# Seven chained attentions on one core: a score slot or a maxima item becomes four heads over both row halves of the array, written to a pair of PSUM banks and drained by one instruction

## The chip, the cores and the metric

One NeuronCore of a Trainium2 chip. The time is device microseconds (us) of one execution, the median of the runs taken; lower is better. TensorE (PE) multiplies, VectorE (DVE) and ScalarE (ACT) read its results out of PSUM, GpSimd (POOL) does small side work, SyncE (SP) issues the DMAs.

## The reference, cut to what matters

Four batches of 256 rows with 160 columns pass through seven attentions and two gated feed-forward blocks. Attentions 0, 2 and 6 read 512 context rows with 20 heads of 8 columns, attentions 1 and 5 are self-attentions over 256 rows with 20 heads of 8, attention 3 reads 508 context rows with 8 heads of 20, and attention 4 has 96 query rows over 256 keys with 8 heads of 20. Each is

```
q = (x @ wq).reshape(b, n, heads, dh).transpose(0, 2, 1, 3)
sim = jnp.einsum('bhid,bhjd->bhij', q, k) * scale
a = jax.nn.softmax(sim, axis=-1)
out = jnp.einsum('bhij,bhjd->bhid', a, v)
x = out @ wo + bo + residual
```

The softmax needs the largest score of each query row and head.

## The kernel before

All work is cut into steps, and `plan()` writes one order of 3015 steps for all engines before the program is built. Each engine walks that order and takes its own part of each step, with semaphores between the engines. `simulate()` makes the order greedily: it keeps a model clock for each engine (`cost()`), due times that are counted in score slots (`PV_LAG`, `K_LEAD`, `M_LEAD`, `FIRST_W`, `BG_LEAD`, `TAIL`), and looks ahead 12 us before it lets TensorE change its shape.

Heads are handled in quads of four. For a quad there are:

- `max` steps (L1024 on PE, L1504 on DVE): scores with the queries as rows of the result, into one bank of 512 fp32 columns; DVE reduces the bank to the row maxima `mx`. With 512 or 508 keys one head fills a bank, with 256 keys two heads do. There are 720 such steps.
- `negm` and `mtr` (L1518, L1519, L1038, L1528): the negated maxima are transposed and added to the query rows, so that the scores of the next step come out already lowered.
- `st` steps, the score slots (L1004 on PE, L1326 on ACT): transposed scores of two heads, 128 keys by 256 queries each, into one bank; ACT writes their exp to one of `N_P = 8` slots of `probs`. There are 736.
- `pv` steps (L1064): four heads' probabilities of a 128-key chunk times the values, into the eighth bank `pv_ps`; `oev` (L1335) reads that out. There are 368 `pv` steps of eight matmul records each.

Heads of a quad lie two on partitions 0 to 63 and two on 64 to 127 (`half`, `same_half`). Score and maxima matmuls contract over 64 rows only, so each uses one half of the array's rows, and matmuls on the two halves can run at once. All heads of one `st` or one `max` step are of the same half, and successive steps alternate halves.

TensorE thus works in three shapes: "rows" (`st` and `max`, 64-row halves), "columns" (`pv`, four 32-column groups) and "full" (all else: projections, transposes, feed-forward, `mtr`). Seven banks `bank_ps` are shared by all steps but `pv`: the planner gives each step any of the seven (`banks_of`), the drain of the step frees it (`bank_taken`), and PE waits for that before it writes the bank again (`take`).

Before the first matmul of an `st` or `max` step, and thus behind a mode change or not, PE waits for its bank:

```python
                def take(step):

                    b, k = turn[step]
                    if k:
                        pe.wait_ge(bank_taken[b], k)
                    return bank_ps[b], bank_full[b]
```

Of the kernel before, what the change touches and what calls it, by code (L numbers as in the profile page):

```python
# [38 lines left out]
P = 128  # L39
# [26 lines left out]
N_P = 8  # L66
RING = 4
RUN = 1
PV_LAG = 2
FIRST_W = 3  # L70
K_LEAD = 4
TAIL = 40
BG_LEAD = 11
M_LEAD = 8
# [128 lines left out]
def plan():  # L203

    quads, slots, span = [], [], []
    for ph, us in enumerate(PHASES):
        for b in range(B):
            first = len(slots)
            for u in us:
                a = ATT[u]  # L210
                n_c = -(-a["nk"] // P)
                for qd in range(a["H"] // 4):
                    n, start = len(quads), len(slots)
                    for c in range(n_c):
                        for k, heads in enumerate(same_half(u, qd)):
                            slots.append(dict(n=n, u=u, b=b, c=c, heads=heads, last=c == n_c - 1 and k == 1))
# [34 lines left out]
    for k in range(len(PHASES) * B):  # L251
        ph, b = divmod(k, B)
        lists = before(ph, b)
        spread(span[k - 1][0] - lead if k else -80, span[k][0] - lead, spread_lists(lists))
# [49 lines left out]
def cost(step, quads):  # L304
# [17 lines left out]
    if kind == "max":  # L322
        rows = a["hpm"] * nk
        return 0.455 * rows, [("dve", 60 + 1.05 * rows)]
# [4 lines left out]
    if kind == "st":  # L329
        return 0.458 * a["hps"] * a["nq"], act(a["hps"] * a["nq"])  # L330
# [38 lines left out]
PATIENCE = 800  # L369
OTHERS = 0.1  # L370
# [13 lines left out]
def simulate(quads, slots, due, stages):  # L384
# [38 lines left out]
    def data_needs(step):  # L423
# [13 lines left out]
        if kind == "st":  # L437
            s = step[1]
            return [("mtr", slots[s]["n"])] + ([pv_of[s - N_P]] if s >= N_P else [])
# [52 lines left out]
    def facts(step):  # L492

        if step not in info:
            pe, after = cost(step, quads)
            side = None
            if step[0] == "st":
                side = half(slots[step[1]]["u"], slots[step[1]]["heads"][0])
            if step[0] == "max":
                side = half(quads[step[1]]["u"], quads[step[1]]["items"][step[2]][2][0])  # L500
            shape = "rows" if step[0] in ("st", "max") else "columns" if step[0] == "pv" else "full"
            info[step] = (needs(step), pe, after, shape, side, takes_buffer(step), due.get(step, (-10**6, 0, 0)), banks_of(step))
        return info[step]

    class State:
# [34 lines left out]
        def choices(self):  # L540

            out = []
            for step, home in list(self.firsts()):
                need, pe, _, shape, side, lock, rank, banks = facts(step)
# [6 lines left out]
                else:  # L551
                    free = seen = max(self.clock["pe"], self.lanes[side] if shape == "rows" else max(self.lanes))
                bank = None
                if banks:
                    open_at = [(0 if self.banks[i] is None else self.at(self.banks[i]), i) for i in banks]
                    open_at = [x for x in open_at if x[0] is not None]
# [3 lines left out]
                    t, bank = max(ready) if ready else min(open_at)  # L560
# [4 lines left out]

        def take(self, choice):

            _, start, free, home, step, bank = choice
            _, pe, after, shape, side, lock, _, _ = facts(step)
# [23 lines left out]
            if bank is not None:  # L593
                self.banks[bank] = ("low", step) if step[0] in LOW else step
# [39 lines left out]
BANKED = SPARE | {"st", "max"}  # L634


def banks_of(step):

    return range(N_BANK) if step[0] in BANKED else ()

# [25 lines left out]
def build(nc, io):  # L666
    order, place, quads, slots = plan()

    value, seen, turn, uses = {}, {}, {}, N_BANK * [0]
    for step in order:  # L670
# [7 lines left out]
        if step[0] in BANKED:  # L678
            turn[step] = (place[step], uses[place[step]])
            uses[place[step]] += 1  # L680

    with ExitStack() as ctx:
# [8 lines left out]
        bank_ps = [ctx.enter_context(nc.psum_tensor(f"bank_ps{i}", [P, 512], F32)) for i in range(N_BANK)]  # L691
# [58 lines left out]
        probs = sb("probs", [P, N_P, 512])  # L750
        gate = sb("gate", [P, FC, SQ])
# [1000 lines left out]
```

## Time and profile before

| | |
|---|---|
| median of 3 runs | 930.72 us (930.34 to 931.19) |
| the profiled execution: its own time | 930.49 us |
| its span, first to last instruction | 928.7 us |
| around the span | 1.8 us |
| PE / DVE / ACT busy | 874.5 / 690.4 / 655.9 us |
| mean granted TensorE clock | 0.98 |

A busy share is a union of overlapping records: matmul records overlap each other, so a PE that is busy for 94% can still be held up between two matmuls. How far it is held up is read from the starts of successive matmuls in the timeline.

### The profile page before, as it was taken

Reading aid. Unit: us, or ns where it says so; the run is one execution under the profiler, and the core shown is the slowest. Engines: PE = TensorE matmul, PEld = TensorE weight load, DVE = VectorE, ACT = ScalarE, POOL = GpSimd, SP = SyncE. Lnnn points to the kernel's source line nnn. Section 1 sums busy time; section 2 is a strip of 40 time slices with the busy share of each in tenths; the row PEclk is TensorE's granted clock in tenths of the full one; section 3 lists DMA queues with packets and bytes.
Section 4 is the critical chain, followed back from the end, with each engine's and each line's share of the span. In section 5 each row is a group of like instructions: output and inputs, shape, how many; then the busy total and the mean of one; then the engine's idle time right before and its main releaser. Section 6 shows DMA issues by size and latency. Waiting matters only on the chain.

```text
span 928.7 us, 21290 instructions
## 1 busy us (share of the span) xinstructions
PE 874.5 (94%) x7810; PEld 592.9 (64%) x7810; DVE 690.4 (74%) x1653; ACT 655.9 (71%) x1419; POOL 56.3 (6%) x98
## 2 busy tenths in 40 slices
PE   8999999999999998989999899999899999898986
PEld 6656655666666666666667666666666656556664
DVE  4978888878888875866867676867788978586813
ACT  8777786877777866776768586677777767667551
POOL 2000000000001000000000000000000000000100
PEclk9999999999999999999999999999999999989989
DMA  8111221111111110111000200101112111111000
GB/s 244 38 38 36 66 58 35 25 29 25 27 38 35 35 28 20 24 35 24 12 2 2 75 2 1 24 18 47 53 28 53 25 36 35 31 23 40 15 8 8
DMA packets 26829, 32.55 MB, mean 35 GB/s; under 512 B 9316, under 2 KB 17768, under 8 KB 26728
## 3 DMA queue, kind: packets, MB, share of 16 engines
q1 hardware_dynamic: 26728, 31.19, 13.3%
q8 instruction: 65, 1.06, 0.5%
q14 instruction: 36, 0.29, 0.1%
HBM read 9.54 MB, written 0.66 MB: 11 GB/s over the span
## 4 chain that ended last, share of the span: by engine, by line
PE 72%; ACT 11%; DVE 10%; issue 5%; SPq 1%; DMA 0%; ACTq 0%; POOL 0%; POOLq 0%; DVEq 0%
PE pv_ps L1064 16%; PE bank_ps L1024 12%; PE bank_ps L1004 10%; ACT probs L1326 5%; DVE mx L1504 5%; PE bank_ps L1111 5%; PE bank_ps L980 4%; PE bank_ps L981 4%; PE bank_ps L1193 3%; PE bank_ps L1091 3%; PE bank_ps L1038 3%; PE bank_ps L1241 3%; PE bank_ps L1181 2%; PE bank_ps L1230 2%; ACT L1439 1%
## 5 line engine op out<-in xcount | busy, mean ns | idle before, releaser
L1504 DVE TENSOR_REDUCE mx<-bank_ps 128x1 f32<-128x512 f32 (+3 forms) x720 | 452.8, 682 | 80.3 <-PE bank_ps L1024 78.7
L1326 ACT ACTIVATE probs<-bank_ps 128x512 f32<-128x512 f32 x736 | 381.1, 605 | 108.8 <-PE bank_ps L1004 107.0
L1064 PE MATMUL pv_ps<-probs,v_all 128*9 128x256 f32 (+2 forms) x2944 | 202.0, 378 | 4.1 <-ACT probs L1326 2.5
L1024 PE MATMUL bank_ps<-ring,qT 64*128 64x512 f32 (+1 forms) x800 | 170.2, 402 | 7.9 <-issue 3.3
L1004 PE MATMUL bank_ps<-qT,ring 64*128 64x256 f32 x1280 | 170.9, 305 | 2.3 <-DVE qT L1528 0.7
L1004 PEld LDWEIGHTS bank_ps<-qT,ring 64*128 64x128 f32 x1280 | 129.8, 186 | 51.3 <-issue 18.8
L1024 PEld LDWEIGHTS bank_ps<-ring,qT 64*128 64x128 f32 x800 | 88.2, 186 | 59.2 <-issue 29.9
L1064 PEld LDWEIGHTS pv_ps<-probs,v_all 128*9 128x9 f32 (+2 forms) x2944 | 57.6, 91 | 75.8 <-issue 21.4
L1377 ACT ACTIVATE kdense<-bank_ps 128x512 fp32r<-128x512 f32 (+2 forms) x116 | 58.7, 560 | 22.6 <-PE bank_ps L1111 22.5
L1111 PE MATMUL bank_ps<-identr,ks 128*128 128x128 f32 (+1 forms) x416 | 61.0, 281 | 8.1 <-DVE gate L1617 4.6
L1301 ACT ACTIVATE ks<-bank_ps 128x320 fp32r<-128x320 f32 x80 | 35.7, 446 | 46.4 <-PE bank_ps L1091 25.3
L1528 DVE TENSOR_TENSOR qT<-bank_ps,qT 128x256 fp32r<-128x256 f32 (+1 forms) x108 | 47.2, 437 | 23.9 <-PE bank_ps L1038 23.3
L1111 PEld LDWEIGHTS bank_ps<-identr,ks 128*128 128x128 f32 (+1 forms) x416 | 52.2, 191 | 17.5 <-DVE gate L1617 4.9
L1335 ACT ACTIVATE oT<-pv_ps 128x256 f32<-128x256 f32 x108 | 43.4, 402 | 22.4 <-PE pv_ps L1064 22.1
L1038 PE MATMUL bank_ps<-identr,mn 128*128 128x128 f32 (+1 forms) x248 | 53.3, 302 | 1.9 <-DVE mn L1519 1.0
L1038 PEld LDWEIGHTS bank_ps<-identr,mn 128*128 128x128 f32 (+1 forms) x248 | 37.9, 192 | 26.8 <-issue 9.5
L1230 PE MATMUL bank_ps<-hx,up 128*128 128x256 f32 x320 | 44.1, 290 | 4.8 <-DVE qT L1528 2.8
L1230 PEld LDWEIGHTS bank_ps<-hx,up 128*128 128x128 f32 x320 | 40.0, 190 | 8.9 <-DVE qT L1528 3.0
L1193 PE MATMUL bank_ps<-ident,oT 128*128 128x128 f32 x216 | 35.6, 300 | 10.2 <-ACT oT L1335 10.1
L1682 POOL TENSOR_SCALAR rstd<-mv 128x2 f32<-128x2 f32 x24 | 5.2, 217 | 657.8 <-DVE mv L1550 657.8
L1605 DVE TENSOR_TENSOR x<-bank_ps,xb 128x320 f32<-128x320 f32 x30 | 14.7, 490 | 33.1 <-PE bank_ps L1241 20.2
L1426 ACT ACTIVATE qT<-bank_ps 128x512 fp32r<-128x512 f32 (+1 forms) x68 | 34.0, 552 | 6.6 <-PE bank_ps L1181 6.1
(188 smaller groups left out, 1032.5 us busy)
## 6 DMA issues: line engine op xcount, KB each, us to landing
ring<-kdense SPq DMA_DIRECT2D x240, 64.0 KB, 2.0
ring<-kdense SPq DMA_DIRECT2D x160, 32.0 KB, 1.9
gate<-in_w_up SPq DMA_DIRECT2D x4, 640.0 KB, 4.4
wb<-in_w_blk SPq DMA_DIRECT2D x2, 960.0 KB, 5.3
wd<-in_w_down SPq DMA_DIRECT2D x2, 400.0 KB, 5.5
x<-in_x SPq DMA_DIRECT2D x4, 160.0 KB, 4.2
bias<-in_bias SPq DMA_DIRECT2D x1, 640.0 KB
out_rows<-x SPq DMA_DIRECT2D x4, 160.0 KB, 1.9
```

Of the source, the lines that this page charges most:

```text
L1004: mm = pe.matmul(bank[0:kr, i * a["nq"]:(i + 1) * a["nq"]], key_op(n, h)[:, c * P:c * P + kr], query_rows(u, b, h), start=True, stop=True)
L1024: mm = pe.matmul(bank[0:rows, j * a["nk"]:(j + 1) * a["nk"]], query_rows(u, b, h)[:, tt * P:tt * P + rows], key_op(n, h)[:, 0:a["nk"]], st ...
L1038: mm = pe.matmul(bank[:, k * a["nq"] + i * P:k * a["nq"] + i * P + rows], m, identr[0:rows, 0:rows], start=True, stop=True)
L1064: mm = pe.matmul(pv_ps[32 * j:32 * j + a["dh"] + 1, 0:a["nq"]], v, probs[0:kr, s % N_P, i * a["nq"]:(i + 1) * a["nq"]], start=(c == 0), st ...
L1111: mm = pe.matmul(bank[:, k * SQ + t * P:k * SQ + t * P + kr], ks[0:kr, t, g * of(u):(g + 1) * of(u), :].rearrange("p h s -> p (h s)"), ide ...
L1193: mm = pe.transpose(bank[0:rows, k * P:(k + 1) * P], src, ident[:, :])
L1230: mm = pe.matmul(bank[:, k * SQ:(k + 1) * SQ], up[:, w, lo:lo + P], hx[:, h, :], start=(j == 0), stop=(j == len(terms) - 1))
L1326: nc.scalar.activation(probs[0:kr, s % N_P, 0:w], bank[0:kr, 0:w], ACT.Exp, scale=float(a["dh"]) ** -0.5).then_inc(free, 1)
L1335: nc.scalar.activation(dst, pv_ps[:, 0:ATT[u]["nq"]], ACT.Copy).then_inc(S["out_taken"], 1)
L1377: nc.scalar.activation(dst, bank[:, 0:n * SQ].rearrange("p (g k) -> p g k", g=n)[:, :, 0:w], ACT.Copy).then_inc(free, 1)
L1504: nc.vector.tensor_reduce(mx[b][0:rows, t, heads[0]:heads[-1] + 1:heads[-1] - heads[0] or 1], bank[0:rows, 0:a["hpm"] * a["nk"]].rearrange ...
L1528: nc.vector.tensor_tensor(q, bank[:, 0:(g1 - g0) * nq], q.bitcast(F32), ALU.add).then_inc(done, 1)
```

## The change

A score slot and a maxima item now hold both halves: `slots` get `heads=same_half(u, qd)`, two lists of two heads, and `items_of` gives for each row tile one item with heads of both halves. So there are 368 `st` and 360 `max` steps in place of 736 and 720, each with twice the matmuls. The matmuls are issued alternately to half 0 and half 1, half 0 into the first bank of a pair and half 1 into the second. The seven banks are three pairs and a lone one; `st` and `max` may only go to a pair, and need both of its banks free, while every other step takes any single bank, by preference the lone one or one whose partner is in use (`alone`). One exp of two times 512 columns and one maximum over two banks drain a pair. `probs` holds the same bytes, as four double slots. On PE, `take` waits for the last user of each of the two banks; each bank's last matmul raises the same semaphore, which is waited for at two more. The due-time constants are halved, since they count slots. The number and the form of the matmuls stay, `pv` too.

```diff
-PV_LAG = 2
-FIRST_W = 3
-K_LEAD = 4
-TAIL = 40
-BG_LEAD = 11
-M_LEAD = 8
+N_D = 4
+N_PAIR = 3
+PV_LAG = 1
+FIRST_W = 2
+K_LEAD = 2
+TAIL = 20
+BG_LEAD = 6
+M_LEAD = 4
...
-    per = [[(t, rows, hs[i:i + a["hpm"]]) for i in range(0, 2, a["hpm"]) for t, rows in tiles] for hs in same_half(u, qd)]
-    return [item for both in zip(per[1], per[0]) for item in both]
+    return [(t, rows, i, [hs[i:i + a["hpm"]] for hs in same_half(u, qd)]) for i in range(0, 2, a["hpm"]) for t, rows in tiles]
...
-                        for k, heads in enumerate(same_half(u, qd)):
-                            slots.append(dict(n=n, u=u, b=b, c=c, heads=heads, last=c == n_c - 1 and k == 1))
+                        slots.append(dict(n=n, u=u, b=b, c=c, heads=same_half(u, qd), last=c == n_c - 1))
...
-        return 0.455 * rows, [("dve", 60 + 1.05 * rows)]
+        return 0.455 * rows, dve(2 * rows)
...
-        return 0.458 * a["hps"] * a["nq"], act(a["hps"] * a["nq"])
+        return 0.458 * a["hps"] * a["nq"], act(2 * a["hps"] * a["nq"])
...
-                if shape == "rows":
-                    self.lanes[side], self.clock["pe"] = t, begin + (pe / 2 if step[0] == "st" else 0)
-                else:
-                    self.lanes, self.clock["pe"] = [t, t], t
-                self.work += pe / 2 if shape == "rows" else pe
+                self.lanes, self.clock["pe"] = [t, t], t
+                self.work += pe
...
+        def alone(self, i, t):
+
+            if i >= 2 * N_PAIR:
+                return True
+            other = self.banks[i ^ 1]
+            return other is not None and (self.at(other) or LATE) > t
...
-    return range(N_BANK) if step[0] in BANKED else ()
+    return range(0, 2 * N_PAIR, 2) if step[0] in DOUBLE else range(N_BANK) if step[0] in BANKED else ()
+
+
+def banks_used(step, i):
+
+    return (i, i + 1) if step[0] in DOUBLE else (i,)
...
-                    b, k = turn[step]
-                    if k:
-                        pe.wait_ge(bank_taken[b], k)
-                    return bank_ps[b], bank_full[b]
+                    for owner in owners[step]:
+                        taken(pe, owner)
+                    return bank_of(step), bank_full[place[step]]
...
-                        for i, h in enumerate(sl["heads"]):
-                            mm = pe.matmul(bank[0:kr, i * a["nq"]:(i + 1) * a["nq"]],
-                                           key_op(n, h)[:, c * P:c * P + kr], query_rows(u, b, h),
-                                           start=True, stop=True)
-                        mm.then_inc(full, 1)
+                        for i in range(2):
+                            for k in range(2):
+                                h = sl["heads"][k][i]
+                                mm = pe.matmul(bank[0:kr, k, i * a["nq"]:(i + 1) * a["nq"]],
+                                               key_op(n, h)[:, c * P:c * P + kr], query_rows(u, b, h),
+                                               start=True, stop=True)
+                                if i == 1:
+                                    mm.then_inc(full, 1)
...
-                        nc.scalar.activation(probs[0:kr, s % N_P, 0:w], bank[0:kr, 0:w], ACT.Exp,
+                        nc.scalar.activation(pair_probs[0:kr, s % N_D, :, 0:w], bank[0:kr, :, 0:w], ACT.Exp,
                                              scale=float(a["dh"]) ** -0.5).then_inc(free, 1)
...
-                        nc.vector.tensor_reduce(mx[b][0:rows, t, heads[0]:heads[-1] + 1:heads[-1] - heads[0] or 1],
-                                                bank[0:rows, 0:a["hpm"] * a["nk"]].rearrange("p (h k) -> p h k", k=a["nk"]),
+                        qd, hpm = quads[n]["qd"], a["hpm"]
+                        m = mx[b][0:rows, t, 4 * qd:4 * qd + 4].rearrange("p (s j) -> p s j" if a["sr"] == 32 else "p (j s) -> p s j", s=2)
+                        nc.vector.tensor_reduce(m[:, :, i:i + hpm], bank[0:rows, :, 0:hpm * a["nk"]].rearrange("p s (h k) -> p s h k", k=a["nk"]),
                                                 AX.X, ALU.max).then_inc(free, 1)
```

## Rows read from the trace of the kernel before

**Rows 1.** The page, busy time of each engine: us, share of span, instructions.

```profile
PE 874.5 (94%) x7810; PEld 592.9 (64%) x7810; DVE 690.4 (74%) x1653; ACT 655.9 (71%) x1419; POOL 56.3 (6%) x98
```

**Rows 2.** The page, chain that ended last, shares of the span.

```profile
PE 72%; ACT 11%; DVE 10%; issue 5%; SPq 1%; DMA 0%; ACTq 0%; POOL 0%; POOLq 0%; DVEq 0%
PE pv_ps L1064 16%; PE bank_ps L1024 12%; PE bank_ps L1004 10%; ACT probs L1326 5%; DVE mx L1504 5%; PE bank_ps L1111 5%; PE bank_ps L980 4%; PE bank_ps L981 4%; PE bank_ps L1193 3%; PE bank_ps L1091 3%; PE bank_ps L1038 3%; PE bank_ps L1241 3%; PE bank_ps L1181 2%; PE bank_ps L1230 2%; ACT L1439 1%
```

**Rows 3.** PE timeline, whole span, first and last score or maxima run: start us, us.

```profile
23.08 1.75 PE L1024 MATMUL bank_ps<-ring,qT 64*128 64x512 f32 x8 [0.57 <-issue]
...
900.30 0.95 PE L1004 MATMUL bank_ps<-qT,ring 64*128 64x256 f32 x4
```

**Rows 4.** PE timeline, undisturbed score or maxima runs and the row behind each.

```profile
252.21 0.50 PE L1004 MATMUL bank_ps<-qT,ring 64*128 64x256 f32 x2
252.64 0.40 PE L1064 MATMUL pv_ps<-probs,v_all 128*9 128x256 f32 x4
...
506.96 0.50 PE L1004 MATMUL bank_ps<-qT,kdense 64*128 64x256 f32 x4
507.39 0.41 PE L1064 MATMUL pv_ps<-probs,v_all 124*21 124x256 f32 x4
...
680.09 0.74 PE L1004 MATMUL bank_ps<-qT,ring 64*128 64x256 f32 x8
680.76 0.40 PE L980 MATMUL bank_ps<-wb,hT_in 128*128 128x160 f32 x1
```

**Rows 5.** PE timeline, a run of seven slots and items, and the row behind.

```profile
836.27 0.74 PE L1004 MATMUL bank_ps<-qT,ring 64*128 64x256 f32 x8
836.85 0.84 PE L1024 MATMUL bank_ps<-ring,qT 64*128 64x512 f32 x3
837.96 0.40 PE L1064 MATMUL pv_ps<-probs,v_all 128*9 128x256 f32 x4 [0.27 <-ACT oT L1335]
```

**Rows 6.** PE timeline, two visits to `pv` (one and three steps), each with the row behind.

```profile
146.58 0.62 PE L1064 MATMUL pv_ps<-probs,v_all 128*9 128x256 f32 x8
147.13 0.39 PE L1004 MATMUL bank_ps<-qT,ring 64*128 64x256 f32 x2
...
99.06 1.48 PE L1064 MATMUL pv_ps<-probs,v_all 128*9 128x256 f32 x24
100.47 0.39 PE L1004 MATMUL bank_ps<-qT,ring 64*128 64x256 f32 x2
```

**Rows 7.** Lines by form, drains: busy us, mean ns | idle before, releaser.

```profile
L1326 ACT ACTIVATE probs<-bank_ps 128x512 f32<-128x512 f32 x688 | 364.1, 617 | 102.7 <-PE bank_ps L1004 101.1
L1326 ACT ACTIVATE probs<-bank_ps 128x192 f32<-128x192 f32 x32 | 9.3, 339 | 5.6 <-PE bank_ps L1004 5.6
L1504 DVE TENSOR_REDUCE mx<-bank_ps 128x1 f32<-128x512 f32 x480 | 301.2, 683 | 48.2 <-PE bank_ps L1024 47.0
L1528 DVE TENSOR_TENSOR qT<-bank_ps,qT 128x256 fp32r<-128x256 f32 x100 | 41.7, 417 | 22.6 <-PE bank_ps L1038 22.1
L1528 DVE TENSOR_TENSOR qT<-bank_ps,qT 128x512 fp32r<-128x512 f32 x8 | 5.5, 687 | 1.3 <-PE bank_ps L1038 1.2
```

**Rows 8.** Timelines of DVE and ACT, drains one behind another.

```profile
49.70 3.67 DVE L1504 TENSOR_REDUCE mx<-bank_ps 128x1 f32<-128x512 f32 x6
...
377.60 3.06 ACT L1326 ACTIVATE probs<-bank_ps 128x512 f32<-128x512 f32 x6
```

**Rows 9.** Views of L1326 and L1504, who waited for it: us, times (largest).

```profile
  PEld bank_ps L1024: 12.7, 24
  PEld bank_ps L1004: 11.0, 31
  PEld pv_ps L1064: 9.1, 27
...
  PEld bank_ps L1004: 9.8, 26
  PEld bank_ps L1024: 9.1, 22
```

**Rows 10.** View of L975, PE's waits that stand as instructions of their own: ns min/median/max.

```profile
L975 PEldq EVENT_SEMAPHORE  x232: 51/51/3063, 21.7 to 894.7; - x116
```

More of the change, by code:

```diff
@@ L369 @@
 PATIENCE = 800
+LATE = 10**9
 OTHERS = 0.1
@@ L495, in facts @@
             pe, after = cost(step, quads)
[L496 to L500, printed above, removed]
             shape = "rows" if step[0] in ("st", "max") else "columns" if step[0] == "pv" else "full"
-            info[step] = (needs(step), pe, after, shape, side, takes_buffer(step), due.get(step, (-10**6, 0, 0)), banks_of(step))
+            info[step] = (needs(step), pe, after, shape, takes_buffer(step), due.get(step, (-10**6, 0, 0)), banks_of(step))
         return info[step]
@@ L543, in choices @@
             for step, home in list(self.firsts()):
-                need, pe, _, shape, side, lock, rank, banks = facts(step)
+                need, pe, _, shape, lock, rank, banks = facts(step)
                 times = [self.at(x) for x in need]
@@ L551, in choices @@
                 else:
-                    free = seen = max(self.clock["pe"], self.lanes[side] if shape == "rows" else max(self.lanes))
+                    free = seen = max(self.lanes)
                 bank = None
                 if banks:
-                    open_at = [(0 if self.banks[i] is None else self.at(self.banks[i]), i) for i in banks]
-                    open_at = [x for x in open_at if x[0] is not None]
+                    open_at = [(max(0 if self.banks[j] is None else self.at(self.banks[j]) or LATE for j in banks_used(step, i)), i) for i in banks]
+                    open_at = [x for x in open_at if x[0] < LATE]
                     if not open_at:
@@ L559, in choices @@
                     ready = [x for x in open_at if x[0] <= max(start, seen)]
-                    t, bank = max(ready) if ready else min(open_at)
+                    t, bank = max(ready, key=lambda x: (self.alone(x[1], max(start, seen)), x)) if ready else min(open_at)
                     start = max(start, t)
@@ L564, in choices @@
             return out
+        def alone(self, i, t):
[3 more added lines that the diff above has]
+            return other is not None and (self.at(other) or LATE) > t
         def take(self, choice):
             _, start, free, home, step, bank = choice
-            _, pe, after, shape, side, lock, _, _ = facts(step)
+            _, pe, after, shape, lock, _, _ = facts(step)
             if home[0] == "stream":
@@ L593, in take @@
             if bank is not None:
-                self.banks[bank] = ("low", step) if step[0] in LOW else step
+                for j in banks_used(step, bank):
+                    self.banks[j] = ("low", step) if step[0] in LOW else step
         def worth(self, choice):
@@ L678, in build @@
         if step[0] in BANKED:
-            turn[step] = (place[step], uses[place[step]])
-            uses[place[step]] += 1
+            b = place[step]
+            turn[step] = (b, uses[b])
+            uses[b] += 1
+            fills[b] += 2 if step[0] in DOUBLE else 1
+            full_at[step] = fills[b]
+            owners[step] = [user[j] for j in banks_used(step, b) if j in user]
+            for j in banks_used(step, b):
+                user[j] = step
     with ExitStack() as ctx:
@@ L690, in build, with bank_of @@
         pv_ps = ctx.enter_context(nc.psum_tensor("pv_ps", [P, 512], F32))
-        bank_ps = [ctx.enter_context(nc.psum_tensor(f"bank_ps{i}", [P, 512], F32)) for i in range(N_BANK)]
+        pair_ps = [ctx.enter_context(nc.psum_tensor(f"pair_ps{i}", [P, 2, 512], F32)) for i in range(N_PAIR)]
+        lone_ps = [ctx.enter_context(nc.psum_tensor(f"lone_ps{i}", [P, 512], F32)) for i in range(N_BANK - 2 * N_PAIR)]
+        bank_ps = [pair[:, i, :] for pair in pair_ps for i in range(2)] + [lone[:, :] for lone in lone_ps]
+        def bank_of(step):
+            return pair_ps[place[step] // 2] if step[0] in DOUBLE else bank_ps[place[step]]
         wm = sb("wm", [P, 2, 640])
@@ L936, in _ @@
                         if before is not None:
[L938 to L939 removed]
+                            scored = ("st", quads[before]["slots"][-1])
+                            sp.wait_ge(bank_full[place[scored]], full_at[scored])
                         for j in range(4):
@@ L1011, in _ @@
                         a = ATT[u]
-                        t, rows, heads = quads[n]["items"][i]
+                        t, rows, _, heads = quads[n]["items"][i]
                         if i == 0:
@@ L1283, in filled @@
             def filled(eng, step):
-                b, k = turn[step]
-                eng.wait_ge(bank_full[b], k + 1)
-                return bank_ps[b], bank_taken[b]
+                b = place[step]
+                eng.wait_ge(bank_full[b], full_at[step])
+                return bank_of(step), bank_taken[b]
             def high_slots(stack, t0, t1, rows, dh, which):
```

38 lines of the change are left out of this document (21 added, 17 removed).

## The prediction

> **What bounds the kernel now.** I read the engines' busy time first, then the chain of work that ended last, then TensorE's timeline. No engine is full: PE has 94%, DVE 74%, ACT 71% [rows 1]. The chain spends 72% of the span on PE, 11% on ACT and 10% on DVE, and the two drains that the change touches, exp (L1326) and maximum (L1504), have 5% each of it [rows 2]. So the order in which PE is fed decides, and most of a gain must come from PE's own time or from its waits for banks.
>
> PE's time in the "rows" shape is in its timeline. I split the timeline wherever PE leaves `st` and `max` for another shape. That gives 310 runs (the first and the last are shown [rows 3]), with 235 visits to `pv` and 219 stretches of full shape between them. From the first matmul of each run to the first matmul behind it the 310 runs take 314 us together. What an undisturbed run costs is seen in three of them: one slot alone takes 0.43 us (252.21 to 252.64), two slots on different halves also 0.43 (506.96 to 507.39), four slots 0.67 (680.09 to 680.76) [rows 4]. So a run costs 0.195 us once, and 0.235 us for each two slots that lie on different halves; **an odd slot costs as much as a pair**, since the other half of the array stands idle. Of the 310 runs 154 have an odd number of slots and items (26 have one, 29 three, 37 five, 55 seven, 6 nine, 1 thirteen). Taking for each run the fuller half, in units of 512 columns, gives 806 units; both halves always full would be 718.
>
> The 314 us are then 310 x 0.195 = 60 us of entering, 718 x 0.235 = 169 us of work with both halves, 88 x 0.235 = 21 us for the idle halves, and 64 us left, which are waits for banks. A run of seven shows them: by these numbers it should take 0.195 + 4 x 0.235 = 1.14 us and takes 1.69 (836.27 to 837.96) [rows 5].
>
> **The change part by part, against the profiled execution** (930.5 us with the 1.8 around its 928.7 us span; the median is 0.2 above it, so the same sum holds for the median).
>
> *Both halves in every step.* The 88 units of idle half go: -20.7 us. This is PE's own time, not hidden by anything: PE's order is one stream. Where a run ended in a wait for a bank the gain is swallowed; where not, it counts in full. I take it in full here and put the waits below.
>
> *One drain for two banks.* In a row of six, a maximum follows the last at (3.67 - 0.68) / 5 = 0.598 us and an exp at (3.06 - 0.61) / 5 = 0.491 us [rows 8]. No row shows a drain of 1024 columns. The nearest rows give the cost of further columns: exp (617 - 339) / 320 = 0.87 ns each, DVE (687 - 417) / 256 = 1.05 ns each [rows 7]. A double exp in a row is then at most 491 + 512 x 0.87 = 936 ns in place of 982, a double maximum 598 + 540 = 1138 in place of 1196. Alone, without a drain ahead of it, the double exp is 617 + 445 = 1062 against 617 + 491 = 1108. So each engine gains some 50 ns a pair: 368 x 0.05 = 18 us of ACT and 360 x 0.058 = 21 us of DVE. Only what is on the chain counts: 5% and 5% of 928.7 are 46 us each, and 5% of these is -4.6 us together. The bounds are 0 (the second bank's columns cost a restart) and -9 (all waits of PE for these drains shrink as well [rows 9]). A double drain begins no later than now: the two matmuls of a slot on one half take 0.235 us in series, and the four of a double, two on each half, take the same.
>
> The Trainium skill (ScalarE: Activation LUTs, the passage on the length of an ACTIVATE) gives 186 ns + 0.833 ns a column and an overlap of 93 ns back to back. That is 613 ns for 512 columns, and the trace has 617. By it a pair of exps in a row would save 93 ns rather than 46, and the sum would be about 2 us lower; the sum keeps the rows.
>
> *Banks in pairs.* This is the debit side. A double holds both banks until the whole drain ends, where now the first bank is free one drain earlier (0.49 or 0.60 us). A full-shape step that sits in one bank of a pair makes the partner useless to `st` and `max`. With three pairs no run can hold more than three doubles without waiting, against seven slots now; 78 of the 310 runs have seven or more. The due planner reacts by leaving the shape earlier, which means more runs. One more run costs 0.195 us to enter, and the visit it splits costs another entry: `pv` takes 0.55 us for one step (146.58 to 147.13) and 1.41 for three (99.06 to 100.47), so 0.43 a step and 0.12 an entry [rows 6]. One more run is therefore about 0.32 us. Now there are 1456 / 2 / 310 = 2.35 pairs a run. The lower bound for the price is no more runs (a mean of 2.35 doubles fits under three). The upper one is a mean of 1.75, 416 runs, +106 x 0.32 = +34 us. I take 25 more runs, a mean of 2.17, +8 us: nearer to the lower end because the runs of one odd slot go and because the halves' waste was in the long runs too. The 64 us of waits I leave as they are, since faster drains and scarcer banks pull opposite ways; one fifth either way, 13 us, is for the range.
>
> The Trainium skill (TensorEngine Tiling (Array Packing), PSUM Bottleneck and Gotcha 1) speaks against the change: tiling speeds up the array, not the emptying of PSUM, and row tiling raises the pressure on banks since the halves must write different ones. The 64 us of waits agree. By that rule alone the 21 us would turn into waits; what this does here is the third rival.
>
> *Waits on PE.* Each `st` and `max` now waits for two banks, so one wait more of the kind that stands as an instruction of its own. 232 such exist at the first step of a quad, 51 ns at the median [rows 10]; about 500 more come. At a median of 51 ns the wait itself is already over when it is reached, and it can be passed while earlier matmuls still run. Cost between 0 and 500 x 0.051 = +25 us; I take +2.
>
> *Hidden.* ACT and DVE get fewer instructions and waits, `pv`, `mtr`, projections and feed-forward keep their matmuls. The ring's DMAs on SP wait for the last score slot of the quad four earlier as now. The constants are halves of the old ones in slots that are twice as large, so the leads stay; I cost them at nothing, and if a lead came out short the chain would show `mx` or `ring` waits at quad starts. `probs` keeps its bytes.
>
> **Sum**: 930.5 - 20.7 - 4.6 + 8 + 2 = 915.2; I say 915.
>
> **The rivals.**
> 1. *Waits shrink as well* (12%). PE records waits for exp and maxima in front of L1024, L1004 and L1064 of 9 to 13 us each [rows 9]. If fewer, larger drains and an exact lane model cut them, and no runs are added: 930.5 - 20.7 - 9 - 13 = 888 at the far end, 895 typically. For it: the old order was partly made of slots that used one half. Against it: pairs are scarcer than banks.
> 2. *The idle halves were free* (16%). Where a run ends because the next bank is taken, a half slot less only lengthens the wait. With the shorter time eaten up by 60 more runs, or by waits, the result is 926 to 934. For it: the 64 us of waits lie mostly in the long runs, 40 us in those of six and more. Against it: the 55 runs of one or three slots show almost no wait, 4 us.
> 3. *Bank pairs run out* (17%). Full-shape steps leave only two usable pairs, runs shrink under 1.9 doubles, and PE switches shape more often. It decides from 25.3 / 0.32 = 79 more runs, 389 in all, 1.87 doubles a run; at 1.75 and with the waits up by a fifth it is 930.5 - 25.3 + 34 + 2 + 13 = 954, typically 942. This is the one that ends slower.
> 4. *The second wait is exposed* (5%). 500 x 0.051 us where PE has eight instructions to issue in the 0.235 us of a double: 915 + 23 = 938.
>
> **How the numbers follow.** The forecast has 50%, with its own range of 903 to 926 (the bounds of the drains, 0 to 50 more runs, half of the waits' fifth). The rivals have 12, 16, 17 and 5%. A range of 893 to 943 leaves out a little of rivals 1 and 3, some 15%. Faster by over 0.2% (below 928.9) takes the forecast, rival 1 and a part of rival 2: 0.63. Within 0.2%, about what a measurement of this kernel can tell from no change: 0.08. Slower: the rest of rival 2, with rivals 3 and 4: 0.29.
>
> **What the profile after would show.** Right: the undisturbed run with one double at 0.43 us and with two at 0.67; no run with L1004 x2 or a lone L1024 of 512 columns; 310 to 360 runs, together under 300 us; exp near 1.05 us and maximum near 1.22 us each, ACT and DVE busy time 15 to 25 us lower each; PE's span share up. Wrong: more than 389 runs, or the time of the runs at 314 us or more, with PE waiting for `probs` or `mx` (rival 2 or 3); gaps of 0.05 us and more behind the extra wait instructions inside a run (rival 4). The forecast falls if the planner cannot keep two doubles a run.

## The result, and the profile after

The changed kernel takes 951.31 us (948.42 to 955.60, four runs) against 930.96 us (930.34 to 932.01) before: a ratio of 1.0221, 95% interval 1.0181 to 1.0262. It is slower, where faster was forecast; whether by more than 2% the interval leaves open. 951 lies outside the range. The profiled execution took 951.76 us with a span of 950.0.

The page after, busy time and chain:

```profile
PE 869.3 (92%) x7810; PEld 566.9 (60%) x7810; DVE 669.8 (71%) x1293; ACT 638.4 (67%) x1051; POOL 56.4 (6%) x98
...
PE 72%; ACT 11%; DVE 10%; issue 6%; DMA 1%; SPq 0%; POOLq 0%; DVEq 0%; ACTq 0%; POOL 0%
```

Against [rows 1, 2] every engine has less to do (DVE -20.6 us, ACT -17.5) and the span is 21 us longer, so each waits more: PE's idle time, its span less its busy time, is 80.7 us against 54.2. The chain's shares have hardly moved, which already says that they were a poor guide to what an engine's time is worth.

PE's timeline, first the undisturbed runs that answer to [rows 4] with the row behind each (one double of maxima, two doubles of slots), then the first and last run:

```profile
563.84 0.49 PE L1048 MATMUL pair_ps<-kdense,qT 64*128 64x508 f32 x2
564.26 0.54 PE L1117 MATMUL pair_ps<-wc,ctxT 128*128 128x320 f32 x1
...
272.79 0.74 PE L1025 MATMUL pair_ps<-qT,ring 64*128 64x256 f32 x8
273.46 0.40 PE L1090 MATMUL pv_ps<-probs,v_all 128*9 128x256 f32 x4
...
22.90 0.50 PE L1048 MATMUL pair_ps<-ring,qT 64*128 64x512 f32 x2 [0.46 <-DMA ring<-kdense]
...
922.04 0.50 PE L1025 MATMUL pair_ps<-qT,ring 64*128 64x256 f32 x4
```

A double takes 0.42 us, two take 0.67, as predicted. There are 356 runs (112 of one double, 125 of two, 114 of three, 5 longer) with 257 visits to `pv` and 245 stretches of full shape from the first run on. The spans between first matmuls, by shape (before has 218 stretches of full shape by this count; the prediction had 219):

| | before | after | |
|---|---|---|---|
| 310 / 356 score and maxima runs | 314.2 us | 305.9 | -8.3 = -20.7 idle halves, +9.0 entries, +3.4 other (waits inside) |
| 235 / 257 visits to `pv` | 192.3 | 214.1 | +21.8, of which 22 x 0.12 = 2.6 are entries |
| 218 / 245 stretches of full shape | 396.1 | 404.1 | +8.0 |

The gain is where it was looked for. Of the signs named beforehand two did not come: the runs take 305.9 us and not under 300, and PE's share of the span fell from 94% to 92%. The loss is in the *other* shapes: by this count a visit to `pv` reaches to the first matmul behind it, and where that is a double that waits for its pair, the wait is counted there. The worst such place, in the timelines of PE, ACT and DVE:

```profile
858.36 0.64 PE L1256 MATMUL pair_ps<-hx,up 128*128 128x256 f32 x4
...
858.92 1.05 PE L1090 MATMUL pv_ps<-probs,v_all 128*9 128x256 f32 x16
859.42 1.27 ACT L1465 ACTIVATE gate<-gate 128x1280 f32<-128x1280 f32 x1
...
860.80 0.87 DVE L1644 SCALAR_TENSOR_TENSOR gate<-pair_ps,cols,gate 128x256 f32<-128x256 f32 x2 [4.88 <-ACT gate L1465]
...
861.92 0.86 DVE L1644 SCALAR_TENSOR_TENSOR gate<-lone_ps,cols,gate 128x256 f32<-128x256 f32 x2
862.71 0.47 DVE L1644 SCALAR_TENSOR_TENSOR gate<-pair_ps,cols,gate 128x256 f32<-128x256 f32 x1
...
863.33 0.79 PE L1025 MATMUL pair_ps<-qT,ring 64*128 64x256 f32 x4 [3.35 <-DVE gate L1644]
```

The feed-forward's `ff_a` results sit in single banks of pairs until the gelu is done; the next score double needs a whole pair, and PE stands idle for 3.35 us. Such long ones are few, and the feed-forward is not the main cause: PE's recorded idle time right in front of a score or maxima run adds up to 4.0 us before and 20.6 after, of which the trace puts 6.2 down to maxima, 6.1 to exps and 6.1 to the feed-forward's L1644. The Trainium skill (TensorEngine Tiling (Array Packing), PSUM Bottleneck and Gotcha 1) holds that tiling speeds up the array and not the emptying of PSUM, and that it raises the pressure on banks; this trace agrees, with the 12.3 us of waits for maxima and exps. Counted more widely, gaps of over 0.04 us beyond the undisturbed change of shape add up to 41 us before and 67 after; of these the ones in front of a score or maxima run go from 9.3 us (40 places) to 29.8 (92 places).

**The clock.** The granted clock is 0.971 in the profiled run after, 0.980 before. TensorE drops from 2.4 to 1.2 GHz in stretches of 3.4 to 6.8 us before and 3.4 to 10.2 after, 37.5 and 54.6 us in all. The windows of the last 130 to 150 us, after and before (PE, PEld, DVE, ACT, POOL busy us and instructions, then granted clock):

```profile
800.00:950.00 150.00, 123.84 (x1034) 81.40 (x1033) 83.28 (x158) 78.16 (x104) 7.83 (x12) 0.91 0.10 23
```

```profile
800.00:928.70 128.70, 109.55 (x910) 75.33 (x910) 73.19 (x173) 70.00 (x136) 7.84 (x12) 0.93 0.09 23
```

In both, PE is busy for only 83 to 85% there and the clock is lowest; elsewhere it is busy for 92 to 96% with a clock of 0.96 to 1.00. **Span times granted clock** turns out to be the steadier measure of a kernel here: 19 executions of before on one chip, with clocks from 0.970 to 0.989, lay between 920.7 and 938.8 us, and their product between 907.5 and 912.2. The two slowest of them, 934.9 and 938.8 us, count as slow and are left out from here on; the median product of the other 17 is 909.0. After has 922.9 (921.5 to 924.8). By this measure 13.9 us of the loss is work and waits, and the rest, some 7 us, goes with the lower clock. I call this product "at full clock" below and use it to tell parts apart, beside the times.

It is a yardstick and not a time that any run took, and it has a lean. Over the 19 executions the span falls by 8.5 us for each 0.01 of clock, where a constant product would want 9.5, so a kernel whose clock is 0.02 lower comes out some 2 us too good (an estimate). Nor does it say what lowers the clock: if a kernel's own waits do, the lost time is its cost all the same.

### The profile page after: what moved, and what is told of

Its sections match the earlier page's. It is cut to its first block, busy times and chain, and to the rows that moved or that the text cites. A ratio compares the mean times of both kernels' runs of the same rounds, so it can differ in the third digit from the quotient of the medians.

```text
span 950.0 us, 20809 instructions
## 1 busy us (share of the span) xinstructions
PE 869.3 (92%) x7810; PEld 566.9 (60%) x7810; DVE 669.8 (71%) x1293; ACT 638.4 (67%) x1051; POOL 56.4 (6%) x98
## 4 chain that ended last, share of the span: by engine, by line
PE 72%; ACT 11%; DVE 10%; issue 6%; DMA 1%; SPq 0%; POOLq 0%; DVEq 0%; ACTq 0%; POOL 0%
PE pv_ps L1090 15%; PE pair_ps L1048 11%; PE pair_ps L1025 11%; DVE mx L1532 6%; ACT probs L1352 5%; PE lone_ps L999 3%; PE pair_ps L1137 3%; PE lone_ps L1267 2%; PE lone_ps L1000 2%; PE pair_ps L1117 2%; PE lone_ps L1137 2%; PE pair_ps L1207 2%; PE pair_ps L1219 2%; PE lone_ps L1256 1%; PE pair_ps L1063 1%
## 5 line engine op out<-in xcount | busy, mean ns | idle before, releaser
L1532 DVE TENSOR_REDUCE mx<-pair_ps 128x2 f32<-128x1024 f32 (+3 forms) x360 | 430.0, 1218 | 110.0 <-PE pair_ps L1048 107.9
L1352 ACT ACTIVATE probs<-pair_ps 128x1024 f32<-128x1024 f32 x368 | 360.2, 1003 | 158.9 <-PE pair_ps L1025 157.8
L1048 PE MATMUL pair_ps<-ring,qT 64*128 64x512 f32 (+1 forms) x800 | 145.0, 405 | 20.1 <-DVE mx L1532 5.7
L1025 PE MATMUL pair_ps<-qT,ring 64*128 64x256 f32 x1280 | 143.2, 313 | 17.9 <-DVE gate L1644 7.8
L1025 PEld LDWEIGHTS pair_ps<-qT,ring 64*128 64x128 f32 x1280 | 102.2, 189 | 77.9 <-issue 36.4
L1048 PEld LDWEIGHTS pair_ps<-ring,qT 64*128 64x128 f32 x800 | 70.6, 187 | 76.7 <-issue 42.9
L1403 ACT ACTIVATE kdense<-pair_ps 128x512 fp32r<-128x512 f32 (+2 forms) x69 | 34.4, 538 | 13.9 <-PE pair_ps L1137 13.7
L1137 PE MATMUL pair_ps<-identr,ks 128*128 128x128 f32 x244 | 37.6, 284 | 1.1 <-DVE mx L1532 0.4
L1137 PEld LDWEIGHTS pair_ps<-identr,ks 128*128 128x128 f32 x244 | 32.3, 196 | 4.5 <-DVE mx L1532 2.3
L1137 PE MATMUL lone_ps<-identr,ks 128*128 128x128 f32 (+1 forms) x172 | 30.0, 293 | 0.7 <-DVE ks L1493 0.7
L1063 PEld LDWEIGHTS lone_ps<-identr,mn 128*128 128x128 f32 (+1 forms) x118 | 17.7, 190 | 19.8 <-issue 13.3
```

The source lines that it names most:

```text
L1025: mm = pe.matmul(bank[0:kr, k, i * a["nq"]:(i + 1) * a["nq"]], key_op(n, h)[:, c * P:c * P + kr], query_rows(u, b, h), start=True, stop=True)
L1048: mm = pe.matmul(bank[0:rows, k, j * a["nk"]:(j + 1) * a["nk"]], query_rows(u, b, h)[:, tt * P:tt * P + rows], key_op(n, h)[:, 0:a["nk"]], ...
L1063: mm = pe.matmul(bank[:, k * a["nq"] + i * P:k * a["nq"] + i * P + rows], m, identr[0:rows, 0:rows], start=True, stop=True)
L1137: mm = pe.matmul(bank[:, k * SQ + t * P:k * SQ + t * P + kr], ks[0:kr, t, g * of(u):(g + 1) * of(u), :].rearrange("p h s -> p (h s)"), ide ...
L1352: nc.scalar.activation(pair_probs[0:kr, s % N_D, :, 0:w], bank[0:kr, :, 0:w], ACT.Exp, scale=float(a["dh"]) ** -0.5).then_inc(free, 1)
L1403: nc.scalar.activation(dst, bank[:, 0:n * SQ].rearrange("p (g k) -> p g k", g=n)[:, :, 0:w], ACT.Copy).then_inc(free, 1)
```

## The experiments

Each is timed beside before on the same chip, in four groups: e1 to e4; e5, e6, b1 and a1; f0, f2, fa and e7; e8 to e10. The table's row of before is that of the second group; at full clock before had 911.0, 909.0, 909.5 and 908.9 in the four. Median time, ratio to before with its interval, and the median at full clock:

| | form | us | ratio | clock | full clock |
|---|---|---|---|---|---|
| before | | 930.1 | | 0.980 | 909.0 |
| after | pairs, held, one drain | 951.3 | 1.022 (1.018-1.026) | 0.971 | 922.9 |
| e1_adjacent | any neighbours, held, one drain | 952.7 | 1.025 (1.018-1.032) | 0.975 | 927.4 |
| e2_halves_only | any two, own release, two drains | 946.6 | 1.017 (1.011-1.023) | 0.959 | 906.1 |
| e3_two_drains | pairs, held, two drains | 972.3 | 1.046 (1.040-1.051) | 0.965 | 935.6 |
| e4_one_wait | after with one wait | 946.5 | 1.018 (1.014-1.022) | 0.973 | 918.3 |
| e5_any_two_held | any two, held, two drains | 939.7 | 1.012 (1.009-1.016) | 0.976 | 917.9 |
| e6_pairs_own | pairs, own release, two drains | 943.0 | 1.012 (1.003-1.020) | 0.982 | 923.6 |
| b1_patience | before, another order | 924.8 | 0.994 (0.991-0.997) | 0.982 | 905.1 |
| a1_patience | after, nearly the same order | 951.9 | 1.021 (1.015-1.027) | 0.971 | 922.9 |
| e7_halves_patience | e2, another order | 949.7 | 1.023 (1.019-1.027) | 0.959 | 908.5 |
| f0_before_short | before, short drains | 883.9 | 0.951 (0.947-0.956) | 0.987 | 870.0 |
| f2_halves_short | e2, short drains | 889.9 | 0.954 (0.946-0.961) | 0.971 | 862.8 |
| fa_after_short | after, short drains | 892.0 | 0.961 (0.958-0.963) | 0.981 | 874.0 |
| e8_ff_banks | after, `ff_a` in the last three banks | 955.8 | 1.025 (1.017-1.033) | 0.971 | 926.1 |
| e9_ff_banks_one_wait | e8 with one wait | 949.5 | 1.021 (1.015-1.027) | 0.970 | 918.5 |
| e10_any_two_one_wait | e5 with one wait | 935.7 | 1.006 (1.002-1.010) | 0.981 | 915.6 |

**Which part costs.** The first group.

e1: the double's banks are any two neighbours of the seven; the planner's rule for which free bank to prefer is fitted to that.

```diff
+                    if step[0] in DOUBLE:
+                        when = {i: x for x, i in open_at}
+                        open_at = [(max(when[i], when[i + 1]), (i, i + 1)) for i in range(N_BANK - 1) if i in when and i + 1 in when]
...
```

> The changed kernel with any two neighbouring banks of the seven for a double (six positions in place of three) and still one drain for both. If it is the fixed pairing of banks that costs the time (theory A), the waits in front of a score or maxima run fall and the time comes to 935 to 945 us. If it is that two banks are held together for the length of a double drain, wherever they lie (theory B), or the planner's order with steps twice as large (theory C), it stays at 945 to 955. Its planned order has 361 score and maxima runs against 356.

e2: any two banks, each with its own drain and semaphores.

```diff
-                        nc.scalar.activation(pair_probs[0:kr, s % N_D, :, 0:w], bank[0:kr, :, 0:w], ACT.Exp,
-                                             scale=float(a["dh"]) ** -0.5).then_inc(free, 1)
+                        for k, (at, count) in enumerate(turn[step]):
+                            act.wait_ge(bank_full[at], count + 1)
+                            nc.scalar.activation(pair_probs[0:kr, s % N_D, k, 0:w], bank_ps[at][0:kr, 0:w], ACT.Exp,
+                                                 scale=float(a["dh"]) ** -0.5).then_inc(bank_taken[at], 1)
...
```

> Only the first half of the change: a slot or item has four heads on both array halves, but in any two of the seven banks, each with its own drain of 512 columns and its own semaphores, so that a bank is free as soon as its own drain ends. Theories A and B (banks in pairs, held together) expect 912 to 930 us, the gain of the full halves without its price. Theory C (larger steps make a worse order) expects 945 or more. 329 runs are planned.

e3: the order and banks of after, two drains (the maximum likewise).

```diff
+                        for k in range(2):
+                            ins = nc.scalar.activation(pair_probs[0:kr, s % N_D, k, 0:w], bank[0:kr, k, 0:w], ACT.Exp,
+                                                       scale=float(a["dh"]) ** -0.5)
+                        ins.then_inc(free, 1)
...
```

> The changed kernel in the very same order and banks, but each double drained by two instructions of 512 columns, the pair freed behind the second. It measures what one drain for two banks gives: by the 46 to 58 ns a pair of the prediction and a chain share of 10 to 11% for the two drains the time should be 5 to 10 us above the changed kernel, 956 to 961 us. If the double instruction were slower than two (theory D), it would be below 951.

e4: the order and banks of after, no wait twice.

```diff
-            owners[step] = [user[j] for j in banks_used(step, b) if j in user]
+            owners[step] = list(dict.fromkeys(user[j] for j in banks_used(step, b) if j in user))
```

> The changed kernel in the same order and banks, but where both banks of a pair were last used by the same step, PE waits once and not twice. If the extra wait instructions hold PE up (rival 4 of the prediction), some us come off, up to 0.051 us for each wait left out; theories A to C expect no change, 948 to 954 us.

e1 brought nothing, so three fixed positions are no worse than six neighbouring ones, and theory A as it was worded for e1 (fixed positions) falls. e2 surprised: with free banks and own release it still takes 946.6 us. At full clock it is 2.9 under the table's before (4.9 under the 911.0 of its own group); its clock is the lowest of all, 0.959. Its stretch from 100 to 200 us shows it, and before's beside it:

```profile
100.00:200.00 100.00, 90.57 (x772) 51.70 (x768) 72.18 (x162) 65.98 (x138) 3.58 (x6) 0.85 0.13 32
```

```profile
100.00:200.00 100.00, 96.82 (x912) 59.45 (x904) 80.50 (x187) 74.58 (x157) 3.51 (x6) 1.00 0.18 45
```

e2's longest stretch at 1.2 GHz is 23.9 us, and in the 6.8 us ahead of it PE was busy for 4.23:

```profile
130.30:137.10 6.80, 4.23 (x46) 1.89 (x38) 6.70 (x13) 2.45 (x5) 0.00 (x0) 1.00 0.18 41
137.10:161.00 23.90, 22.30 (x132) 13.56 (x136) 14.02 (x27) 12.22 (x25) 0.00 (x0) 0.50 0.10 23
```

But the clock is not all that e2 loses. The busy times on its page:

```profile
PE 870.2 (92%) x7810; PEld 568.3 (60%) x7810; DVE 687.5 (73%) x1653; ACT 654.6 (69%) x1419; POOL 56.6 (6%) x98
```

In its span of 945.6 us PE is idle for 75.4 us, against 54.2 before. Two costs in this are not of the halves as such. First, e2 keeps the second wait of each double: PE's waits that stand as instructions of their own number 965 in before, 1576 in after and 1846 in e2. Second, its order holds one long stop, of which 5.46 us are recorded as idle before a matmul. PE, the view of L995, where PE waits in `take` (its longest wait, 5.96 us, is this one), and SP there:

```profile
358.01 0.62 PE L1092 MATMUL pv_ps<-probs,v_all 128*9 128x256 f32 x8
364.09 1.22 PE L1050 MATMUL all_ps<-ring,qT 64*128 64x512 f32 x4 [5.46 <-issue]
...
L995 PEldq EVENT_SEMAPHORE  x843: 51/51/5963, 22.0 to 906.3; - x169
...
359.75 0.28 SPq L926 DMA_DIRECT2D ca_n<-in_ctx  x1
360.13 4.94 SPq L962 DMA_DIRECT2D ring<-kdense  x8
```

PE needs keys from the ring, and SP issues their transfers only behind a small load of attention 4's context rows (L926), which by SP's program waits until a VectorE step (L1498, 359.41 us) has freed its bank. So a late transfer, and not a bank, stops the kernel there. Before has no idle place of PE over 2.8 us.

e3 showed the single drain to be worth 21 us of time and 12.7 at full clock in this order, several times the forecast. PE's idle time is 90.2 us in it, 80.7 in after. The order was planned with the cost of one drain, so a plan made for two might lose less; that was not tried with pairs held. The busy times on e3's page, then the top two groups by line and form of e3, then those of after (busy us, mean ns of one, idle time before them and its releasers):

```profile
PE 877.4 (91%) x7810; PEld 570.3 (59%) x7810; DVE 692.2 (72%) x1653; ACT 660.6 (68%) x1419; POOL 56.5 (6%) x98
```

```profile
L1353 ACT ACTIVATE probs<-pair_ps 128x512 f32<-128x512 f32 x688 | 366.2, 605 | 144.1 <-PE pair_ps L1025 142.3
L1535 DVE TENSOR_REDUCE mx<-pair_ps 128x1 f32<-128x512 f32 x480 | 301.5, 683 | 60.6 <-PE pair_ps L1048 59.3
```

```profile
L1352 ACT ACTIVATE probs<-pair_ps 128x1024 f32<-128x1024 f32 x344 | 344.4, 1026 | 145.9 <-PE pair_ps L1025 144.9
L1532 DVE TENSOR_REDUCE mx<-pair_ps 128x2 f32<-128x1024 f32 x240 | 286.4, 1218 | 66.9 <-PE pair_ps L1048 65.4
```

ACT's and DVE's busy time differ by 22 us each, as the 18 and 21 of the forecast said; a double exp takes 1.026 us, a double maximum 1.218. The Trainium skill (ScalarE: Activation LUTs, the passage on the length of an ACTIVATE) gives 186 ns + 0.833 ns a column, 1039 ns for 1024 columns; the trace has 1026.

e4 is 4.8 us of time and 4.6 at full clock under after. PE's separate waits of the `taken` helper, after and in e4:

```profile
L896 PEldq EVENT_SEMAPHORE  x1230: 51/51/2952, 10.9 to 943.1; - x176
```

```profile
L896 PEldq EVENT_SEMAPHORE  x737: 51/51/3180, 11.8 to 937.8; - x185
```

493 waits of 51 ns less gave 4.6 us, 9 ns each: most are covered, but not all. After was timed in another group than e4, and before moved by 2 us between groups, so the size is rough; e9 against e8, in one group, gives 7.6 us for 492 waits, 15 ns each. At 9 ns the 881 waits that e2 has more than before would cost some 8 us, an estimate.

**Position or holding, and how much is the order.** The second group. e5 is e2 with both banks given back behind the second drain, e6 is e3 with each bank given back behind its own; the planner reckons with it in both. b1 and a1 change one number of the planner, `PATIENCE = 700`, in before and in after.

> As e2_halves_only (any two of the seven banks, two drains of 512 columns), but both banks are given back together, behind the second drain. If what costs is that the first bank is held through the drain of the second (theory B), the time is near that of e3_two_drains, 962 to 975 us. If it is the fixed pairs (theory A), it is near e2_halves_only, 942 to 952 us. 361 score and maxima runs are planned, against 329 of e2_halves_only.

> As e3_two_drains (fixed pairs of banks, two drains of 512 columns), but each bank is given back behind its own drain, and the planner reckons with that. Theory B expects about what e2_halves_only has, 942 to 952 us; theory A stays near e3_two_drains, 962 to 975 us. 335 runs are planned.

> The kernel before, with the planner's PATIENCE at 700 in place of 800 and nothing else: another order of the same steps (296 score and maxima runs in place of 310). It shows how far two orders of the same kernel lie apart. If the difference between before and after is a lucky order of before (theory C in its strong form), this is some 940 us or more; if the orders are alike, 925 to 937 us.

> The changed kernel with PATIENCE at 700 in place of 800: another order of the same steps (356 runs, as many as after has). If the order of the changed kernel is an unlucky one, this comes to 935 to 943 us; if the loss is in the change itself, 945 to 957 us.

By the times alone e5 and e6 fit neither theory, because e2 and e3, between which they stand, have the lowest clocks. At full clock the four forms with two drains make a square:

| at full clock | own release | held together |
|---|---|---|
| any two banks | 906.1 (e2) | 917.9 (e5) |
| pairs | 923.6 (e6) | 935.6 (e3) |

Holding costs 11.8 and 12.0, pairs 17.5 and 17.7, so both holding and pairing cost, and the two add roughly. That they add to a fifth of a microsecond is luck: counted against before of its own group (e2 -4.9, e5 +8.9, e6 +14.6, e3 +24.6) holding costs 13.8 and 10.0, pairs 19.5 and 15.7. The four also differ in their planned orders (329, 361, 335 and 356 runs), the own-release forms have 270 waits more, and e2 has its stop of 5.46 us. "Pairs" means neighbours: e1 shows that fixed positions are not what costs.

Theory C, the unlucky order, is tested less well than planned. b1 is another order of before (its steps differ from the 536th on) and moves it by 3.9. But a1 is no other order of after: the planner gives the same steps at 2281 of 2287 places, and its 922.9 is after's repeated, 13.9 above before in the same group. e7's order differs from e2's at 291 of 2287 places and moves it by 2.4. What speaks against an unlucky order of after is that other plans with all pairs held are no better: e1 has 927.4 and e8 (350 runs) 926.1.

**Waits or PE's own time.** The third group. In f0, f2 and fa the exp leaves out one of its two heads and the maximum half of the keys, so the drains take about half as long; e7 is e2 with `PATIENCE = 700`.

```diff
+                        w //= 2
...
-                                                bank[0:rows, 0:a["hpm"] * a["nk"]].rearrange("p (h k) -> p h k", k=a["nk"]),
+                                                bank[0:rows, 0:a["hpm"] * a["nk"]].rearrange("p (h k) -> p h k", k=a["nk"])[:, :, 0:a["nk"] // 2],
```

> The kernel before in its own order, but each exp covers only one of its two heads (256 of 512 columns) and each maximum only the first half of the keys; the rest is left out, so that both drains take about half as long (three memsets of some 4 us are added at the start). Only its difference to f2_halves_short and fa_after_short is of interest. If PE waits for drains are a good part of the time, it falls well under before, to 880 to 905 us.

> e2_halves_only with the same halved drains. Theory E: the 21 us of idle halves are truly saved on PE and then given back as waits for ACT and DVE; with short drains the saving shows, and this run is 10 to 20 us under f0_before_short. Theory C (larger steps make a worse order, whatever the drains) expects it above f0_before_short by as much as e2_halves_only is above before, about 16 us.

> The changed kernel with the same halved drains (two times 256 columns an exp, half the keys a maximum). If its loss is waits for banks held through long drains, it is at or under f0_before_short (within 5 us above it at most); if its loss is in PE's own time (more changes of shape, two waits a step), it stays 10 us or more above it.

> e2_halves_only with PATIENCE at 700, another order of the same steps. e2_halves_only had the lowest granted clock of all kernels (0.96). If that belongs to its order and not to its form, this one comes to 920 to 935 us with a clock of 0.975 to 0.985; if it belongs to the form, it stays at 942 to 950. Span times granted clock should be 902 to 910 in either case.

In time f2 is 6 us above f0 and fa 8 us above it, so neither came out as expected: f2 was to be 10 to 20 under, and fa lies between its two cases. At full clock f2 is 7.2 under f0, where e2 is 2.9 under before; after's 13.9 above before shrink to 4.0 (fa above f0). fa and f0 keep the orders of after and before, so about 10 of after's 13.9 us go with the length of the drains. Of the 20.7 us of idle halves 4 more show when the drains are short, less if the product's lean is counted: f2's one execution at a clock of 0.990 has 866.8, only 3.2 under f0. Theory E holds in part only. By an estimate most of the rest is no mystery: f2 has e2's 881 additional waits, some 8 us at 9 ns, and its stop for late keys, 5.0 us there, which with the 7.2 make 20.2 of the 20.7. No run takes either away from the form, so this is not shown. e7 has e2's clock again (0.959), so two orders, alike over most of their length, agree that it goes with the form; which trait of the form does it, I cannot say.

**Is it the feed-forward's banks?** The last group. e8 lets `ff_a` take the last three banks only, e9 adds e4's edit, e10 is e5 with e4's edit.

```diff
+    if step[0] == "ff_a":
+        return range(N_BANK - 3, N_BANK)
```

> The changed kernel, but the feed-forward's up steps ff_a, which hold their bank until the gelu is done, may only take the last three of the seven banks, so that they can block one pair and the lone bank, not two pairs. If steps of full shape that sit long in a pair are what makes fixed pairs dear (theory F), 5 to 10 us come off: 941 to 946 us, and the 20 us that PE's instructions spend waiting for L1644's banks fall by half or more. If the price is spread over all short steps, it stays at 948 to 954.

> e8_ff_banks, and one wait in place of two where both banks of a pair have the same last user. The two are taken to add up: some 5 us under e8_ff_banks, 936 to 941 us, still above before.

> e5_any_two_held (any two of seven banks, two drains, given back together) with the second wait left out where one step used both banks last. If the single wait is worth the same 5 us here, 933 to 937 us. It would show whether any form with both halves in each step reaches the kernel before; none is expected to.

The gain that theory F expected did not come: 926.1 at full clock, 3.2 above after, and it is another order too. The waits for those banks did not go (23.4 us of waits are put down to L1644 in after, 26.6 to its line L1646 in e8), they moved, in the main from the score doubles to the feed-forward itself. The waits of e8 (engine, line, what it waited for: us, times, longest), then of after:

```profile
PEld lone_ps L1258 <- DVE gate L1646: 8.1, 4, 3.1
...
PE lone_ps L1258 <- DVE gate L1646: 7.0, 4, 2.9
...
PEld pair_ps L1050 <- DVE gate L1646: 3.1, 1, 3.1
```

```profile
PE pair_ps L1025 <- DVE gate L1644: 7.8, 3, 3.4
...
PEld pair_ps L1025 <- DVE gate L1644: 5.0, 2, 2.6
...
PE pair_ps L1048 <- DVE gate L1644: 4.2, 2, 2.8
```

e9 is 7.6 under e8 at full clock, e10, with 299 waits fewer, 2.3 under e5. e10 comes nearest of the forms with both halves and is still 0.6% above before. The only version that beats both kernels is b1, before with another order: 924.8 us, 0.994 (0.991 to 0.997).

## Why the prediction was wrong, point by point

- **Both halves in every step, -20.7 us.** Right inside the runs (806 units became 718, and the undisturbed durations hold), wrong as a saving: "I take it in full here". e2 has it without pairs or holding and gains 2.9 us at full clock, 7.2 with short drains, while PE's idle time rises from 54.2 to 75.4 us. Rival 2 had it that the gain turns into waits; that these are waits for the next bank is shown only in part, since e2 also has more wait instructions and one stop for late keys.
- **One drain for two banks, -4.6 us.** The engines' savings were right (18 and 21 forecast, 22 and 22 found). The step that failed is "Only what is on the chain counts", with its bound of -9: it measured -12.7 at full clock and -21 in time. A drain that ends earlier also frees two banks earlier, and with banks scarce that may be worth more than its share of the chain; PE's idle time, 90.2 us with two drains and 80.7 with one, fits this, though the order was planned for one drain.
- **Banks in pairs, +8 us.** This is the step that turned the sign. 46 more runs came, not 25, at 0.32 us each 15 us, within its bounds. But the price was put on the number of runs, and the waits were left "as they are", with only those inside a run counted. Pairs cost 17.6 and holding both banks 11.9 at full clock, the means of the square, and the gaps at changes of shape rose by 26 us where none were priced. Rival 3 named the scarcity of pairs but had its path wrong: it was to act through runs of under 1.9 doubles and to decide from 389 runs. There were 356, with 2.04 doubles each, and the loss came as waits in front of them.
- **Waits on PE, +2 us.** 611 more came (965 became 1576), and 493 of them cost 4.6 us (e4). The prediction counted 232, but those are the ones of one line.
- **The clock** was in no term. Some 7 us went with it.

Set out at full clock the parts are 909.0 - 2.9 (halves, with their waits) + 17.6 (pairs) + 11.9 (held) - 12.7 (one drain) = 922.9. That this is the measured value is no check: the parts are differences along the chain from before over e2 and e3 to after, and must add up. The checks are that holding and pairing each come out alike by two ways, to some 4 us, and that a1 repeats the 13.9 beside before. Another order moved a kernel by 3.9 (b1) and 2.4 us (e7), and before moved by 2 us between groups, so no part is good to better than some 4 us.

What stays open: how much of the missing gain of e2 is its additional waits and its late keys, why e2's form lowers the clock, and which steps make pairs dear. One drain over any two banks was not tried, nor e2 with the keys' transfers ahead of the small load.

## What to carry to other kernels

A buffer that must be free in neighbouring pairs, and is held until the whole pair is drained, can cost more than it gives where work of another kind takes single buffers, and its price is to be sought in front of the runs that need the pairs, not inside them. Price an idle part of an engine at full value only if the engine never waits behind it. Before an experiment is read as one part of a change, count what else it keeps: e2 was to be free of the change's price and still had the second waits and a late transfer. And check that another setting of a planner really gives another plan. Where span times granted clock is steadier than the time, compare kernels by both, or a difference in clock is taken for a difference in work.

## What the runs showed that I had not expected

Nineteen executions of before differed by 2.0% in time and by 0.5% in span times clock. Matmuls on the two row halves ran side by side even where two of the same half followed each other in the stream: four slots, each of two matmuls on one half, took 0.67 us, the same as two doubles issued alternately [rows 4].
